# Layer 0 of a graph kernel: the one-hot becomes the weights of the scatter, and the messages move as two float32r parts

## The reference, cut to what matters

```python
edge_index = jnp.stack([src, dst])
h = jnp.maximum(_layernorm(x), 0.0)
x = x + layer0(h, edge_index, edge_attr_16, ...)
h = jnp.maximum(_layernorm(x), 0.0)
x = x + layer1(h, edge_attr_32, eps, src, dst)

def layer0(x, edge_index, edge_attr, ...):
    row, col = edge_index
    h = jnp.concatenate([x[row], edge_attr], axis=1)
    h = jnp.maximum(h @ w1a + b1a, 0.0)
    h = h @ w1b + b1b
    s = jax.ops.segment_sum(h, col, num_segments=x.shape[0])
    cnt = segment_sum(ones, col)
    agg = s / jnp.maximum(cnt, 1.0)[:, None]
    ...
```

## Time and profile before

| | |
|---|---|
| time, median of 3 runs | 6154.6 us (6152.95 to 6156.02) |
| the profiled execution, its span | 7360.0 us (no other time of it is given) |
| loop of layer 0, from its first scatter to its last window | 98.5 to 3839.5 us of the span |
| loop of layer 1 | 3955.0 to 7338.4 us |
| busy share of the span | PE 87%, PEld 74%, POOL 62%, ACT 59%, VectorE 52% |
| share of the DMA engines busy in the two loops | 0.20 and 0.17 |

### The profile page before, as it was taken

The page is one execution under the profiler, slowest core; times in us unless marked ns, Lnnn a source line. Parts: engine busy times, 40 slices in busy tenths (PEclk is TensorE's granted clock), DMA queues, the critical chain, the costliest instruction groups (busy, mean ns, idle before and its releaser), DMA issues. The chain is left out here.

```text
span 7360.0 us, 107042 instructions
## 1 busy us (share of the span) xinstructions
PE 6429.2 (87%) x32834; PEld 5436.7 (74%) x32835; DVE 3791.4 (52%) x9052; ACT 4370.5 (59%) x8707; POOL 4564.4 (62%) x4834
## 2 busy tenths in 40 slices
PE   7888888888888888888887888888888889888888
PEld 5777777777777777777777777777777777777777
DVE  5343434434444443434446666666666666666666
ACT  5555555555555555555556666666666666666665
POOL 5666666666666666666655666666666666666665
PEclk8999899888898999898998999999999999999999
DMA  3222221222222122222211111111111111111111
GB/s 104 55 55 55 54 54 54 55 55 55 55 56 54 54 55 55 54 54 57 56 44 43 42 44 44 44 39 44 44 42 41 44 44 42 41 44 44 44 39 40
DMA packets 331462, 367.43 MB, mean 50 GB/s; under 512 B 87161, under 2 KB 256536, under 8 KB 331166
## 3 DMA queue, kind: packets, MB, share of 16 engines
q0 software_dynamic: 152000, 160.05, 10.0%
q1 hardware_dynamic: 46276, 130.67, 5.3%
q10 hardware_dynamic: 133146, 76.25, 3.7%
HBM read 358.17 MB, written 8.46 MB: 50 GB/s over the span
## 5 line engine op out<-in xcount | busy, mean ns | idle before, releaser
L1015 PE MATMUL bank<-part_high,owner_hot 125*128 125x448 f32 (+1 forms) x10500 | 4250.6, 405 | 224.1 <-issue 162.9
L1015 PE MATMUL bank<-part_low,owner_hot 125*128 125x448 f32 (+1 forms) x10500 | 4127.5, 393 | 152.6 <-issue 150.9
L986 POOL DMA_INDIRECT gathered<-projected_rows,indices x2500 | 2366.8, 947 | 1412.8 <-issue 705.7
L986 POOL DMA_INDIRECT gathered<-hidden_rows,indices x2250 | 2135.2, 949 | 1277.1 <-issue 854.6
L1015 PEld LDWEIGHTS bank<-part_high,owner_hot 125*128 125x128 f32 x10500 | 2144.2, 204 | 505.2 <-issue 228.8
L1015 PEld LDWEIGHTS bank<-part_low,owner_hot 125*128 125x128 f32 x10500 | 2137.9, 204 | 412.6 <-issue 189.7
L1118 ACT ACTIVATE owner_hot<-owner_in,minus_piece 125x256 fp32r<-125x256 f32 (+2 forms) x3948 | 1591.4, 484 | 128.4 <-remote 69.9
L1261 DVE SCALAR_TENSOR_TENSOR hidden<-window_f,places_now,bank 128x512 f32<-128x512 f32 x1500 | 1104.8, 737 | 1074.6 <-remote 609.0
L1123 ACT ACTIVATE owner_hot<-owner_hot 125x1792 fp32r<-125x1792 f32 (+1 forms) x750 | 1275.5, 1701 | 23.8
L1317 DVE TENSOR_TENSOR sums<-sums,bank 97x48 f32 (+1 forms) x1250 | 244.2, 195 | 1694.6 <-remote 1396.7
L1045 PEld LDWEIGHTS bank<-hidden,messages 128*97 128x97 f32 x6250 | 644.4, 170 | 424.2 <-issue 418.3
(11 more groups left out here) (128 smaller groups left out, 2721.4 us busy)
## 6 DMA issues: line engine op xcount, KB each, us to landing
owner_in<-owner_rows SPq DMA_DIRECT2D x188, 448.0 KB
edges<-in_edge ACTq DMA_DIRECT2D x124, 400.0 KB
gathered<-projected_rows,indices POOLq DMA_INDIRECT x2500
gathered<-hidden_rows,indices POOLq DMA_INDIRECT x2250
hidden<-owner_rows SPq DMA_DIRECT2D x62, 448.0 KB
edges<-in_edge ACTq DMA_DIRECT2D x124, 200.0 KB
projected_rows<-projected SPq DMA_DIRECT2D x25, 168.0 KB
sources<-in_src_cols SPq DMA_DIRECT2D x1, 1562.5 KB, 6.4
```

The lines of the kernel that those rows point to most:

```text
L986: pool.indirect_dma_start(gathered_rows(k, row)[:, t, :], None, table, bass.IndirectOffsetOnAxis(ap=index(k, odd(turn))[:, t:t + 1], axis= ...
L1015: last = nc.tensor.matmul(bank[pick_home[home]][:, 0:PITCH * D].rearrange("p (f b) -> p f b", b=PITCH)[:, :, 0:rows.shape[2]], pick_hot(pi ...
```

## The change

In layer 0 alone the scatter is turned round. The one-hot (128 edges x 48, now float32r) is the weights; the messages move, 194 columns: a high part of 97 and a low part of 97, both float32r, in `parts`. The window then stands in PSUM as 48 nodes x 194. VectorE folds the two halves (`fold`, a reduce) into `window_rows` in SBUF; TensorE turns that (`turn_window`, a transpose) two chunks after, into columns 256 on of the same bank; `add_window` closes three chunks after instead of two.

To make the parts, VectorE copies the picked tile's 96 columns from PSUM into `gathered` (in `add_edges`), masks all 480 columns from `gathered` into `high_rows` (`mask_rows`, SBUF to SBUF) and subtracts (`keep_low_rows`: `gathered` minus `high_rows`, both in SBUF). ACT's `rectify` takes the Relu of both parts, 480 columns each. `mark` now reads the window's numbers from `window_f`, so that both of its tensor inputs lie in SBUF. `mask_rows` waits until ACT has rectified the chunk before, `rectify` until the scatter two chunks before is done. `messages` is no longer there in this loop, and its memsets on POOL are gone; VectorE has six small memsets ahead of the loop.

```diff
@@ sum_near_windows, homes in layer 0 @@
+                parts = [sb(f"parts{n}", [P, TILES, 2 * PART], F32R, scope=scope) for n in range(2)]
+                onehot = [sb(f"onehot{n}", [P, TILES, WINDOW], F32R, scope=scope) for n in range(2)]
+                high_rows = hidden_flat[:, 0:TILES * H1].rearrange("p (t n) -> p t n", n=H1)
+                window_rows = [sb(f"window_rows{n}", [P, PART], scope=scope) for n in range(2)]
...
@@ TensorE @@
                         for t in range(TILES):
-                            last = nc.tensor.matmul(bank[window_home(k, turn)][0:summands, 0:WINDOW],
-                                                    summand(k, t), onehot[k][:, t, :],
-                                                    start=(t == 0), stop=(t == TILES - 1))
+                            if layer == 0:
+                                to, weights, moving = (bank[window_home(k, turn)][0:WINDOW, 0:2 * PART],
+                                                       hot_places(k, turn)[:, t, :], parts[by_twos(k, turn)][:, t, :])
...
+                            last = nc.tensor.matmul(to, weights, moving, start=(t == 0), stop=(t == TILES - 1))
                         last.then_inc(windows, 1)
+                    def turn_window(k, turn):
+                        pe.wait_ge(folded, chunks_before(turn) + (k + 1))
+                        nc.tensor.transpose(bank[window_home(k, turn)][0:PART, TURNED:TURNED + P],
+                                            window_rows[by_twos(k, turn)][:, :], ident[:, :]
+                                            ).then_inc(windows_turned, 1)
...
                                 scatter(slot, earlier)
+                            if layer == 0 and not (first and k < 2):
+                                earlier, slot = at(turn, k - 2)
+                                turn_window(slot, earlier)
@@ ACT, rectify in layer 0 @@
-                            act.wait_ge(added, chunks_before(turn) + (k + SLOTS + 1))
-                            tiles = tiles_in(k, odd(turn))
-                            nc.scalar.activation(message[k][:, TILES - 1, 0:row],
-                                                 bank[edge_home[k]][:, (TILES - 1) * H1:TILES * H1], ACT.Relu)
-                            nc.scalar.activation(message[k][:, 0:tiles, 0:row], gathered_rows(k, row)[:, 0:tiles, :],
-                                                 ACT.Relu).then_inc(rectified, 1)
+                            act.wait_ge(rows_split, chunks_before(turn) + (k + 1))
+                            act.wait_ge(windows, chunks_before(turn) + (k + SLOTS - 1))
+                            part = parts[by_twos(k, turn)]
+                            nc.scalar.activation(part[:, :, 0:row], high_rows, ACT.Relu)
+                            nc.scalar.activation(part[:, :, PART:PART + row], gathered_rows(k, row), ACT.Relu
+                                                 ).then_inc(rectified, 1)
@@ VectorE @@
+                        places_of_window = window_f[:, :] if layer == 0 else ramp[window_home(k, turn)]
                         nc.vector.tensor_tensor(
-                            onehot[k][:, :, :], spread(ramp[window_home(k, turn)], TILES, 1),
+                            hot_places(k, turn)[:, :, :], spread(places_of_window, TILES, 1),
                             spread(offsets_now[:, odd(turn), k, :], WINDOW, 2), ALU.is_equal).then_inc(hot, 1)
...
+                            nc.vector.tensor_tensor(rows, rows, other, ALU.add)
+                            nc.vector.tensor_copy(gathered_rows(k, row)[:, tiles:TILES, :].rearrange("p t n -> p (t n)"),
+                                                  bank[edge_home[k]][:, tiles * H1:TILES * H1]).then_inc(added, 1)
...
+                    def mask_rows(k, turn):
+                        dve.wait_ge(added, chunks_before(turn) + (k + SLOTS + 1))
+                        dve.wait_ge(rectified, chunks_before(turn) + (k + SLOTS))
+                        nc.vector.tensor_scalar(high_rows.bitcast(I32), gathered_rows(k, row).bitcast(I32),
+                                                HIGH_BITS, HIGH_BITS, ALU.arith_shift_right, ALU.logical_shift_left
+                                                ).then_inc(rows_masked, 1)
+                    def keep_low_rows(k, turn):
+                        dve.wait_ge(rows_masked, chunks_before(turn) + (k + 1))
+                        nc.vector.tensor_tensor(gathered_rows(k, row), gathered_rows(k, row), high_rows, ALU.subtract
+                                                ).then_inc(rows_split, 1)
+                    def fold(k, turn):
+                        dve.wait_ge(windows, chunks_before(turn) + (k + SLOTS + 1))
+                        halves = bank[window_home(k, turn)][0:WINDOW, 0:2 * PART].rearrange("w (h c) -> w h c", h=2)
+                        nc.vector.tensor_reduce(window_rows[by_twos(k, turn)][0:WINDOW, :],
+                                                halves.rearrange("w h c -> w c h"), AX.X, ALU.add).then_inc(folded, 1)
...
                             add_edges(k, turn)
                             if layer:
                                 split_rows(k, turn)
+                            else:
+                                mask_rows(k, turn)
                             if closes:
                                 add_window(slot, earlier, base)
+                            if layer == 0:
+                                keep_low_rows(k, turn)
+                                if not (first and k < 2):
+                                    earlier, slot = at(turn, k - 2)
+                                    fold(slot, earlier)
                             mark(k, turn)
```

More of the change, by code:

```diff
@@ L1340, in chunks @@
                         for k in range(SLOTS):
-                            earlier, slot = at(turn, k - 2)
+                            earlier, slot = at(turn, k - CLOSE)
                             closes = k >= skipped
@@ L1369, in _ @@
                     if layer == 0:
+                        for rows in window_rows:
+                            nc.vector.memset(rows[:, :], 0.0)
+                        for part in parts:
+                            nc.vector.memset(part[:, :, H1:PART].bitcast(F32), 1.0)
+                            nc.vector.memset(part[:, :, PART + H1:2 * PART].bitcast(F32), 0.0)
                         dve.wait_ge(w_mean_made, 1)
@@ L1388, in _ @@
                     chunks(LAST, last=True)
-                    for k, base in zip((SLOTS - 2, SLOTS - 1), window_bases(CHUNKS - 2, 2)):
+                    last_bases = window_bases(CHUNKS - CLOSE, CLOSE)
+                    for k, base in zip(range(SLOTS - CLOSE, SLOTS), last_bases):
+                        if layer == 0 and k >= SLOTS - 2:
+                            fold(k, LAST)
                         add_window(k, LAST, base)
@@ L1465, in _ @@
                         act.wait_ge(added, 1)
[L1466 removed]
+                        nc.scalar.activation(message[:, :, 0:row], gathered_rows(0, row), ACT.Relu)
                     @block.vector
```

74 lines of the change are left out of this document (46 added, 28 removed).

## The result

The changed kernel takes 6192.3 us (median of 4 runs, 6188.7 to 6196.5) against 6153.8 for the kernel before (4 runs beside it). The ratio is 1.0063, 95% interval 1.0049 to 1.0077: slower by 38.6 us. The prediction said slower, by 126.

What follows compares the result with a forecast made beforehand. POOL's gathers, 1.248 us each, were taken to bound the kernel (sum 6109 us against a median of 6154.6). Held gathers at 0.20 us x 625 chunks added 126 us, giving 6280 us, range 6030 to 6430.

Steps and rivals of the forecast that it cites:

- Pace: Layer 0: POOL sets the pace, 4 x 1.248 = 4.99 us a chunk against TensorE's 4.74.
- TensorE's terms: Layer 0 chunk: new scatter 0.50 and transpose 0.11 us replace 0.80; 4.74 goes to 4.55, at worst 5.14.
- VectorE and ACT: Layer 0 chunk: VectorE gains 1.55 us, to 3.9; ACT's two activations take 1.16, its average stays under 4.2.
- The term that counts: POOL against VectorE, layer 0: operations with two SBUF inputs hold gathers, 0.20 us a chunk, range 0.02 to 0.45.
- I scale with the square: Layer 0: hit chance and wait both grow with length, so subtraction 9 x 18 ns plus mark 2.25 x 18 ns.
- layer 1's 18 ns: Layer 1's 160-column addition L1295: 5 ns x 2230 gathers / 620 operations = 18 ns of POOL per short operation.
- the locked step: Layer 0: VectorE and POOL run in step, the same gather may meet the subtraction every time; upper end 0.45 a chunk.
- TensorE as the pace: Rival: a timed gather costs 0.94 us, layer 0's chunk follows TensorE from 4.74 to 4.55, 6036 us; chance 0.20.
- No change: Rival: POOL sets the pace and the starts hardly meet, 6155 us within 12; chance 0.10.
- ACT and VectorE binding each other: Rival, layer 0: mask waits for ACT's last `rectify` behind one-hot batches, 2.2 us a turn, +275, 6430 us; chance 0.08.
- Only the mask holds gathers: Rival, layer 0: short subtractions slip through, the mask alone costs 0.04 us a chunk, 6180 us; chance 0.05.
- the rule that the prediction names beside it: Skill page: an addition with two SBUF inputs gets in the way of GpSimd's reads alone; no size given.

Runs made afterwards that it cites:

- the kernel with three gathers: Changed kernel with three of the four gathers of each layer 0 chunk, first tile of every slot zeros: 5974.5 us, ratio 0.9721.
- the second profile of before: The kernel before, unchanged, profiled once more: 6144.6 us (one run), the profile spans 6142.5.
- the version without these operations: Changed kernel with high parts put into the chunk's PSUM bank, subtraction reading them there, mark from PSUM ahead of the fold: 6153.2 us, ratio 1.0006.
- the shorter delay: Kernel before with layer 0's mark from SBUF and two copies of the old mark ahead of it, without the 48-column copy: 6271.0 us, ratio 1.0178.

## Why the prediction was right and wrong

**Pace: right.** POOL's 1.248 us a gather set the pace before and after. The kernel with one scatter matmul (0.9998) and the one with three gathers (-151 us against a spare 0.25 x 625 = 156) show both halves of the reading. That no microsecond saved on TensorE would be seen held.

**TensorE's terms: right.** With three gathers the new scatter takes 2008.22 - 2007.69 = 0.53 us (taken: 0.50), and a chunk without waits 4.45 (4.55). Both come from the kernel with three gathers, where TensorE is nearest to setting the pace.

**VectorE and ACT: right.** Copy, mask, subtraction and fold were taken at 0.20, 0.40, 0.65 and 0.30; they measure 0.25, 0.42, 0.69 and 0.34. ACT's two activations of 480 columns make 1.2 us (1.16).

**The term that counts: that gathers are held is right, its size is wrong.** The failed step is "I scale with the square: 9 x 18 + 2.25 x 18 = 0.20 us a chunk". The held gathers of layer 0 make 29 us, 29 / 625 = 0.05 a chunk. The step took it that each operation meets the gathers at any moment of their step with equal chance, and that layer 1's 18 ns were the price of such an even chance. Both fail.

With the rule that the runs gave, an even chance would make this (an estimate): an operation of length d that must have begun by the time e (after the gather's start; before it counts negative) costs (d - 0.127 + e)^2 / (2 x 1.249) on average. For the subtraction, e = -0.045: 0.095; for the mask 0.023; for the mark with e = 0.22 behind the fold 0.093. The sum of 0.21 lies by the prediction's 0.20, but its parts are not the prediction's 0.16, 0 and 0.04, so that is luck. For layer 1's addition of 0.334 us, whose edge in the second profile of before lies at -0.045 too and whose end counts less 0.136, the same formula gives 0.009 an operation; the 198 gathers that it holds there make 14.7 us, 0.024 an operation. So what was scaled was itself the price of a certain moment.

In layer 0 the moment was a cheap one. VectorE's chunk begins when a gather has landed: 349 of 612 chunks start between 0.05 before and 0.1 after a gather's start. From there to the subtraction it is 2004.61 - 2003.41 = 1.20 us, nearly one step of the gathers. So 407 of 623 subtractions start between 0.05 before and 0.125 after a gather's start, and none of these gathers is held. Moved on together against the gathers, the three operations of this trace would cost between 32 us and 210 (an estimate by the rule, with all steps at 1.249); where the change put them, 39 by the rule and 29 by the gathers' own lengths. The prediction named the locked step as its upper bound alone ("the same gather may meet the subtraction every time"); a lock can just as well miss every time, and the prediction did not work out which it would be. That the change cost 38 us and not 200 is luck.

A part of this luck the gathers themselves bring about. In the changed kernel 102 masks begin 0.54 to 0.75 us after a gather's start; they take up to 0.63 us instead of 0.41, and all end 1.17 to 1.18 us after that start, wherever they began. For example:

```profile
1205.51 0.94 POOL L993 DMA_INDIRECT gathered<-projected_rows,indices  x1 [0.30 <-issue]
1206.75 0.94 POOL L993 DMA_INDIRECT gathered<-projected_rows,indices  x1 [0.30 <-issue]
```

```profile
1206.16 0.53 DVE L1329 TENSOR_SCALAR hidden<-gathered 128x480 int32<-128x480 int32 x1
...
1206.72 0.72 DVE L1336 TENSOR_TENSOR gathered<-gathered,hidden 128x480 f32<-128x480 f32 x1
```

The subtraction behind such a mask then starts 0.03 to 0.045 before the next gather, just too late to hold it. Without the mask's wait the 102 would start earlier and by the rule cost 45 us (an estimate). This is read from the starts and ends in the trace; no run tests it by itself.

**The shares: wrong.** Forecast were 0.16 a chunk for the subtraction, 0.04 for the mark and 0 for the mask, which was put at nothing since no row showed it. Measured: 2.3, 17.8 and 9.0 us in all, so 0.004, 0.028 and 0.014. The order is turned round, since the moment counts and not the length.

**The rivals.** TensorE as the pace fell at once. "No change" has its mechanism in part: most starts do not meet. ACT and VectorE binding each other exists, in the kernel with three gathers, but only below POOL's pace, where it costs nothing. "Only the mask holds gathers" is wrong: in the kernel before with the mark from SBUF and the shorter delay there is no mask, and 479 gathers are held. The Trainium skill, SBUF — State Buffer, section "Who interferes with whom", reports a probe in which two-input operations (tensor_tensor) did not stall such DMAs; the comparisons with two SBUF inputs of that run stalled them by 0.1 to 0.28 us each, so the measurement decides against the probe; it does not speak against the rule that the prediction names beside it, since a gather reads its `indices` from SBUF, and no run here tells reads from writes. Another rule of the same section, that the order of issue and not the shape decides who blocks, agrees with the edge in the table: with the shorter delay all 344 marks that began up to 75 ns before a gather held it, and none of the 80 that began 25 to 175 ns after.

Of the 38.6 us the gathers of layer 0 explain some 30, and the version without these operations can't be told from the kernel before. Layer 1 differs by 7 us between the two profiles. Its own addition, the same in both kernels, holds 198 gathers in one and 212 in the other, 14.7 and 19.2 us. Whether the change moved it to a dearer moment stays open: its gathers have means of 952 and 954 ns in other profiles, too.

No version that does the whole work beat the kernel before. The way to one would be fewer gathers on POOL, and TensorE now has some 0.54 us a chunk to spare (4.99 - 4.45). A sixth pick per turn in layer 0 was not tried; at the 3.00 us a pick that the prediction read from the rows it would ask more of TensorE than the 2.7 of five chunks, so by these numbers it would not pay (an estimate).

## What to carry to other kernels

When one engine's queue sets the pace, add up its own step from start to start, and price every edit by what it does to that step; work saved elsewhere is worth nothing, as one run with most of it left out will show. Where two engines run in step, an average over all moments prices nothing: read from the trace where the operation starts against the one that it can hold, as a delay of a tenth of a microsecond took the same mark from 109 us to 35 here. The safe form is the one that held no gather at any moment: for an operation with two inputs one of them in PSUM, for the mask its result in PSUM. That gave the whole loss back, though VectorE had more to do. A result in PSUM does not save an operation whose two inputs both lie in SBUF, as layer 1's addition shows.

## What the runs showed of the hardware

Two kinds of VectorE operation held indirect gathers on POOL in these runs: those with both inputs in SBUF (the subtraction, the mark, the long additions, and layer 1's addition, which writes to PSUM), and the mask with its one input and its result in SBUF. The gather's end then moves by the operation's end, seen from the gather's start, less 0.12 to 0.14 us (means by operation and run; single gathers 0.11 to 0.14). With one of the two inputs in PSUM, or the mask's result there, no gather was held. Layer 1's addition with a gather, in the second profile of before:

```profile
3498.34 1.08 POOL L986 DMA_INDIRECT gathered<-hidden_rows,indices  x1 [0.30 <-PE bank L1015]
```

```profile
3498.27 0.33 DVE L1295 TENSOR_TENSOR bank<-gathered,edges 128x160 f32<-128x160 f32 x1 [1.71 <-DMA gathered<-hidden_rows,indices]
```

When the gather is first, VectorE pays instead, at two places. Subtractions that start 25 to 50 ns before a gather take 725 ns, those that start 25 ns after it or later 659. And the mask, not the subtraction, waits at a second place: in all five kernels that have this mask, those that begin 0.54 to 0.75 us after the gather's start end 1.17 to 1.19 after it; subtractions that begin there keep their 658 ns.

Not settled: what sets the edge. Mask, subtraction and layer 1's addition must have begun some 0.045 us before the gather. A mark behind reads of PSUM held up to 0.017 after the gather's start, one behind `add_window` 0.034 after it, a mark behind the fold up to 0.22 after. The fold begins 0.27 ahead of that mark, so counted from the fold this edge lies at -0.05 too. The long addition of the earlier trace rows fits that and not the prediction's reading, that a gather is stuck which starts while the addition runs: it began at 119.69, 0.60 after the gather that it held (119.09), and both long gathers end 0.80 after the addition beside them. Ahead of this addition ran a reduction that had begun 0.17 before the gather:

```profile
118.92 0.78 DVE L1242 TENSOR_REDUCE far_max<-fars 1x1 f32<-1x625 int32 x1
119.63 0.13 DVE L1244 TENSOR_SCALAR one_eps<-eps_col 128x1 f32<-128x1 f32 x1
```

A reduction ahead seems to hold the place for what follows it; the fold with a mark from PSUM held nothing of its own. No run tests that.
